# Routing steps at other tiles, the next run's first gathers ahead of the last scatters, and a third bank of line sums, in a fused two-layer mixer kernel

## The reference

```
x = x + _L0_conv_ref(_ln_c(x), ...)      # line convolutions, batch norm, one gate per image and channel
t = t + _L0_ffn_ref(_ln_t(t), ...)       # 8 experts, top 2 of the softmax, gelu (tanh)
x = x + _L1_conv_ref(_ln_c(x), ...)      # max pools of 7 sizes, two of them weighted per channel
t = t + _L1_ffn_ref(_ln_t(t), ...)       # 8 experts, top 2, gelu (erf)
```

## Time and profile before

| | us |
|---|---|
| three runs | 1142.77, 1144.22, 1144.31 |
| the profiled execution | 1153.62 |
| its span, first to last instruction | 1151.9 |
| PE busy | 821.9 (71%) |
| POOL busy | 625.4 (54%) |
| DVE busy | 566.6 (49%) |
| ACT busy | 527.0 (46%) |

### The profile page before, as it was taken

How to read it: one execution, slowest core, us unless ns; L and a number is a source line. 1 busy time by engine, 2 the same in 40 slices (tenths; PEclk the granted TensorE clock), 3 DMA queues, 4 the chain that set the end, 5 groups by cost and what they waited for, 6 DMA issues and landing times.

```text
span 1151.9 us, 14717 instructions
## 1 busy us (share of the span) xinstructions
PE 821.9 (71%) x4289; PEld 696.3 (60%) x4289; DVE 566.6 (49%) x1296; ACT 527.0 (46%) x1439; POOL 625.4 (54%) x598
## 2 busy tenths in 40 slices
PE   1754388887778776877688388776878877877670
PEld 0434267775677565765587277665768755666670
DVE  8877912270500291999557769997571003200004
ACT  1505054453445354544448166443575534444463
POOL 1000255666666674778733645787455666666551
PEclk9975599997988978998879689989887988889795
DMA  7001343442556752444234743444265646546356
GB/s 309 1 0 55 120 152 111 134 151 93 188 152 201 236 176 90 147 132 124 92 95 162 271 153 124 134 119 132 67 201 157 197 123 218 172 132 209 112 159 219
DMA packets 55391, 167.63 MB, mean 146 GB/s; under 512 B 13888, under 2 KB 13901, under 8 KB 55056
## 3 DMA queue, kind: packets, MB, share of 16 engines
q1 hardware_dynamic: 36880, 130.98, 34.0%
q0 software_dynamic: 18432, 35.70, 10.9%
HBM read 137.26 MB, written 31.46 MB: 146 GB/s over the span
## 4 chain that ended last, share of the span: by engine, by line
PE 49%; issue 14%; ACT 10%; another core or an unknown queue 8%; POOL 7%; DVE 6%; DMA 5%; SPq 0%; POOLq 0%; ACTq 0%; DVEq 0%
PE yT_ps L766 17%; PE h_ps L753 17%; PE turn_ps L688 4%; POOL xg L491 4%; DMA xg<-xn_rows,tile_rows 4%; POOL y_rows L500 3%; ACT hT L566 3%; PE acc_ps L705 3%; PE xT_ps L742 2%; ACT work L604 2%; PE yr_ps L776 2%; PE h_ps L851 1%; PE acc_ps L725 1%; ACT yT L577 1%
## 5 line engine op out<-in xcount | busy, mean ns | idle before, releaser
L500 POOL DMA_INDIRECT y_rows<-yr,tile_rows x288 | 313.1, 1087 | 280.3 <-ACT yr L586 201.1
L491 POOL DMA_INDIRECT xg<-xn_rows,tile_rows x288 | 308.1, 1070 | 221.9 <-DVEq L1168 130.1
L753 PE MATMUL h_ps<-xT,expert 128*128 128x256 f32 (+1 forms) x1408 | 321.0, 378 | 64.9 <-issue 47.3
L766 PE MATMUL yT_ps<-hT,expert 128*128 128x256 f32 (+1 forms) x1408 | 309.2, 372 | 40.6 <-ACT yT L577 28.4
L566 ACT ACTIVATE hT<-h_ps,expert 128x256 f32<-128x256 f32 (+1 forms) x704 | 254.8, 449 | 151.1 <-PE h_ps L753 72.8
L753 PEld LDWEIGHTS h_ps<-xT,expert 128*128 128x128 f32 x1408 | 249.0, 213 | 100.2 <-issue 66.8
L766 PEld LDWEIGHTS yT_ps<-hT,expert 128*128 128x128 f32 x1408 | 254.8, 212 | 77.5 <-ACT yT L577 33.4
L1202 DVE SCALAR_TENSOR_TENSOR tok<-work,share,tok 128x128 f32<-128x128 f32 x224 | 61.1, 346 | 328.5 <-DMA work<-y_rows 323.5
L577 ACT ACTIVATE yT<-yT_ps,expert 128x256 f32<-128x256 f32 (+1 forms) x176 | 73.9, 442 | 180.9 <-PE yT_ps L766 104.5
L742 PE MATMUL xT_ps<-ident,xg 128*128 128x128 f32 x288 | 62.7, 302 | 82.8 <-DMA xg<-xn_rows,tile_rows 72.2
L554 ACT ACTIVATE xT<-xT_ps 128x256 f32<-128x256 f32 x144 | 56.1, 390 | 139.7 <-PE xT_ps L742 94.1
(11 more groups left out here) (206 smaller groups left out, 642.7 us busy)
## 6 DMA issues: line engine op xcount, KB each, us to landing
expert<-in_experts SPq DMA_DIRECT2D x176, 514.5 KB
work<-y_rows SPq DMA_DIRECT2D x24, 512.0 KB, 9.5
xn_rows<-work SPq DMA_DIRECT2D x16, 512.0 KB, 2.7
xg<-xn_rows,tile_rows POOLq DMA_INDIRECT x288
y_rows<-yr,tile_rows POOLq DMA_INDIRECT x288
tok<-in_x_tokens SPq DMA_DIRECT2D x8, 512.0 KB, 7.1
state<-in_x SPq DMA_DIRECT2D x2, 2048.0 KB, 17.1
work<-y_rows SPq DMA_DIRECT2D x16, 256.0 KB, 6.0
```

The lines of the kernel that those rows point to most:

```text
L491: pool.indirect_dma_start(xg[:, s, h, :], None, xn_rows[unit], bass.IndirectOffsetOnAxis(ap=tile_rows[unit % 2][:, at, 0, h:h + 1], axis=0)) \
L500: pool.indirect_dma_start(y_rows[unit], bass.IndirectOffsetOnAxis(ap=tile_rows[unit % 2][:, at, 1, h:h + 1], axis=0), yr[:, s, h, :], None ...
L753: mm = pe.matmul(h_ps[c // 2][:, c % 2, cols], expert[:, t.load(h) % W_RING, c * P:(c + 1) * P], xT[:, t.slot(2), cols], start=True, stop= ...
L766: mm = pe.matmul(yT_ps[:, cols], expert[:, t.load(h, d) % W_RING, HIDDEN + c * P:HIDDEN + (c + 1) * P], hT[:, s, c, cols], start=(c == 0), ...
```

## The change

Four things are changed together.

1. **First pass.** ACT normalises groups 3 and 7 of image 0 and groups 1, 4 and 7 of image 1 (`BY_SCALAR`), all of an image ahead of its copies; DVE does the other 11. The product of image 0 with the line weights is no longer reduced by DVE but summed on PE in the bank `yT_ps`, as the column products are; its eight slabs are 8 neighbouring columns of each of the 64 lines. The product of image 1 is still reduced by DVE and now lies in the memory of `expert`.
2. **Drain of a run.** In step 35 PE and ACT take `turn_y` and `copy_rows` of tile 33 and of tile 34, in step 36 those of tile 35; step 37 holds no more work for them.
3. **POOL between the runs.** Tiles 0 and 1 of the next run are gathered in step 36 ahead of the scatters of tiles 34 and 35; tiles 2 and 3 follow after them. The waits for `s_rows` and `s_xn_st` move up with the first two.
4. **The table.** `mixing(0)`: route from 28.6 and 29.3 to 28 and 28.3, slots from 32 to 30.3, rows from 31..34 to 30..33, invert from 35.6..38 to 33..34.3. `mixing(1)`: read from 0 to 2, state and norm two tiles later, route, slots and rows 1.3 to 2.4 tiles later, invert 0.3 to 1.3 tiles later.

```diff
-    mixing(0, read=3, state=(6, 7, 7.6, 8), norm=11, route=(28.6, 29.3), slots=32, rows=(31, 32.6, 33, 34),
-           invert=(35.6, 36.6, 37, 38)),
-    mixing(1, read=0, state=(2, 2.6, 3, 4), norm=5, route=(23.6, 24.3), slots=26.6, rows=(26, 27, 27.6, 28),
-           invert=(29, 30, 30.6, 31)),
+    mixing(0, read=3, state=(6, 7, 7.6, 8), norm=11, route=(28, 28.3), slots=30.3, rows=(30, 31, 31.6, 33),
+           invert=(33, 33.3, 34, 34.3)),
+    mixing(1, read=2, state=(4, 5, 5.6, 6), norm=7, route=(25, 25.6), slots=28, rows=(27.3, 28.6, 29.3, 30),
+           invert=(30.3, 30.6, 31, 31.3)),
...
+    def drains(self):
+        return self.last <= self.s <= self.last + 1
...
+            def begin(u, ahead):
+                pool.wait_ge(s_rows, u + 1)
+                pool.wait_ge(s_xn_st[u], 16 * QUARTERS)
+                for d in ahead:
+                    gather(Tile(u, 0), d)
+
             for u in range(UNITS):
                 if begins_run(u):
-                    pool.wait_ge(s_rows, u + 1)
-                    pool.wait_ge(s_xn_st[u], 16 * QUARTERS)
-                    for d in range(G_AHEAD):
+                    if u == 0:
+                        begin(u, range(G_FIRST))
+                    for d in range(G_FIRST, G_AHEAD):
                         gather(Tile(u, 0), d)
...
+                    if t.s == t.last + 1 and u + 1 < UNITS:
+                        begin(u + 1, range(G_FIRST))
                     if t.has(-2):
                         scatter(t, -2)
...
-                    if t.has(-2):
+                    if t.has(-2) and t.s <= t.last:
                         turn_y(t, -2)
+                    if t.drains():
+                        turn_y(t, -1)
...
+            pe.wait_ge(s_mul, 1)
+            add_slabs(h_ps[0][:].rearrange("p a s -> p (a s)"), lambda g: tok_flat[0][:, g * chunk:(g + 1) * chunk])
+            pe.wait_ge(s_mul, 2)
+            add_slabs(yT_ps[:].rearrange("p (h w) -> p h w", h=SIDE),
+                      lambda g: by_row[0][:, :, g * SIDE // GROUPS:(g + 1) * SIDE // GROUPS])
+            pe.wait_ge(s_mul, 3)
+            add_slabs(h_ps[1][:].rearrange("p a s -> p (a s)"), lambda g: tok_flat[1][:, g * chunk:(g + 1) * chunk])
```

More of the change, by code:

```diff
@@ L59 @@
 G_AHEAD = 4
+G_FIRST = 2
 RUNS = [(0, 1), (2, 3)]
+BY_SCALAR = [(3, 7), (1, 4, 7)]
+BY_VECTOR = sum(GROUPS - len(groups) for groups in BY_SCALAR)
 AFTER_UP, AFTER_DOWN = 0.3, 0.6
@@ L293, in build @@
         yr = sb("yr", [P, RING, HALVES, P])
+        by_row = [m.rearrange("p (h w) -> p h w", h=SIDE)
+                  for m in (work[2][:], expert[:].rearrange("p w e -> p (w e)")[:, 0:TOKENS])]
         def one_hots(u, k):
@@ L647, in _ @@
             for b in range(IMAGES):
-                for g in range(GROUPS + 1):
-                    if g < GROUPS:
-                        if g % 2:
-                            for t in range(g * GROUP, (g + 1) * GROUP):
-                                i = b * BLOCKS + t
-                                ins = act.activation(tok[b][:, t, :], tok[b][:, t, :], ACT.Identity,
-                                                     bias=first_shift[:, i:i + 1], scale=first_rstd[:, i:i + 1])
-                            ins.then_inc(s_ln_odd, 1)
-                    if g:
-                        copy_group(work[b], g - 1)
+                for g in BY_SCALAR[b]:
+                    for t in range(g * GROUP, (g + 1) * GROUP):
+                        i = b * BLOCKS + t
+                        ins = act.activation(tok[b][:, t, :], tok[b][:, t, :], ACT.Identity,
+                                             bias=first_shift[:, i:i + 1], scale=first_rstd[:, i:i + 1])
+                    ins.then_inc(s_ln_act, 1)
+                for g in range(GROUPS):
+                    copy_group(work[b], g)
             turned.n += 2
@@ L832, in _ @@
             mm.then_inc(s_turned, 1)
+            by_scalar = [0]
             def turn_first(b):
                 for g in range(GROUPS):
-                    if g % 2:
-                        pe.wait_ge(s_ln_odd, (b * GROUPS + g + 1) // 2)
+                    if g in BY_SCALAR[b]:
+                        by_scalar[0] += 1
+                        pe.wait_ge(s_ln_act, by_scalar[0])
                     else:
@@ L981, in _ @@
             for b in range(IMAGES):
-                for g in range(0, GROUPS, 2):
+                for g in range(GROUPS):
+                    if g in BY_SCALAR[b]:
+                        continue
                     for t in range(g * GROUP, (g + 1) * GROUP):
@@ L992, in _ @@
                 banks_read(dve, turned.n)
[L993 removed]
+                img, by_h = (m.rearrange("p (h w) -> p h w", h=SIDE) for m in (work[b][:], tok_flat[b]))
                 dve.tensor_tensor(by_h, img, bc(conv_w[:, 0, :].unsqueeze(2), [P, SIDE, SIDE]), ALU.mult).then_inc(s_mul, 1)
[L995 to L1000 removed]
+                ins = dve.tensor_tensor(by_row[b], img, bc(conv_w[:, 1, :].unsqueeze(1), [P, SIDE, SIDE]), ALU.mult)
+                if b == 0:
+                    ins.then_inc(s_mul, 1)
+                else:
+                    op(ins)
+            op(dve.tensor_reduce(lines[:, 1, 1, :], by_row[1], AX.X, ALU.add))
+            summed = ((lines[:, 0, 0, :], h_ps[0][:].rearrange("p a (h w) -> p w (a h)", w=SIDE)),
+                      (lines[:, 1, 0, :], yT_ps[:].rearrange("p (h w) -> p h w", h=SIDE)),
+                      (lines[:, 0, 1, :], h_ps[1][:].rearrange("p a (h w) -> p w (a h)", w=SIDE)))
+            for n, (line, slab) in enumerate(summed):
+                dve.wait_ge(s_sum, n + 1)
+                op(dve.tensor_reduce(line, slab, AX.X, ALU.add))
             for k in range(2):
```

22 lines of the change are left out of this document (7 added, 15 removed).

## The result

| | before | after |
|---|---|---|
| runs, us | 1142.77, 1142.79, 1144.22, 1144.31 | 1125.38, 1126.26, 1127.53, 1127.80 |
| median | 1143.51 | 1126.89 |
| profiled execution, its span | 1153.62, 1151.9 | 1127.53, 1125.8 |

The ratio is 0.985, with a 95% interval of 0.9815 to 0.9884: 16.6 us faster, at 1126.9 where I had forecast 1125. The two traces are 26.1 us apart, since the profiled execution of before was 10 us over its own median and that of after is at its median. The ratios of the experiments leave out the few executions in a second, slower state, and one of `first_only` that took 4156 us.

What follows compares the result with a forecast made beforehand. POOL sets the pace inside a run wherever nothing stalls, with stalls on top, longest at routing steps and between runs. 3.4 - 17 - 5.5 = -19.1 us takes 1151.9 to 1132.8, execution 1134.5; scaled by 0.992, 1125 us, range 1113 to 1137.

Steps and rivals of the forecast that it cites:

- First pass: Image sums at the start: PE becomes the bound with three sums, the third ending at 68.9 against 65.51, +3.4 us.
- The strided sum: First pass, new sum on PE: plain column price taken; rival of 2.3 times the price, +10.1 us, 1135 us, 10 in 100.
- End of run 0: Routing of unit 2 leaves the path: `s_rows` at 614 to 620 instead of 640.1, scatter of tile 33 at 628.
- The rival without stalls: End of run 0: tile 33 scattered at 620, all 8 us earlier, 1117 us; 14 in 100.
- slots at 30.3 answer at once: End of run 0: DVE's slots find the top 2 ready, where it waited 10.03 us for them before.
- POOL and combine: Between the runs: 5.2 us of gathers come in between, combine starts at 647.6 instead of 645.85, costing DVE's chain 1.8 us.
- DVE's result: Unit 2: the result comes 40.6 us after the start of combine instead of 46.8, 6.2 us earlier.
- ACT stays late: Unit 2: the 10.21 us of idle and the stalls of the halves remain, -7.2 us, 1137 us; 12 in 100.
- The 12.4 us for two more tiles: Unit 2: two more tiles are through at DVE's result, 2 x 6.2 = 12.4 us gained.
- the 17: Unit 2 and its start: 12.4 + 6.2 - 1.8 = 17 us gained.
- Routing halves of unit 2: Halves at 25 and 25.6 stall POOL less than at 23.6 and 24.3: 5.5 us gained, bounds 0 and 11.
- End of the kernel and `s_rows` of unit 3: End of the kernel: 0, bounds +0.5 and -0.5; POOL's request for `s_rows` in step 32: 0, at most +2.

Runs made afterwards that it cites:

- before_again: The kernel before, unchanged, profiled a second time; ratio 1.0005 to the kernel before.
- first_only: The kernel before with the new first pass alone (table, drains and POOL of before); ratio 0.9982 to the kernel before.
- mixing0_old: The kernel after with the old table row of unit 1, all else new; ratio 0.9979 to the kernel before.
- no_pool: The kernel after without the early gathers ahead of the scatters of tiles 34 and 35; ratio 0.9837 to the kernel before.
- g_first_4: The kernel after with four tiles of unit 2 gathered ahead of the last scatters instead of two; ratio 0.9886 to the kernel before.

## Why the prediction was right, and where it was not

The sum was -19.1 us. In the table above the means of after's two traces and of those of before (with `first_only` from A on) differ by -1.1 us at the first gather, -6.6 in A, -8.9 in B, -1.9 in C and -1.2 in the last column; the other two are the same within 0.3. The two pairs of spans differ by 19.3 us on average, the timed runs by 16.6. The total is right and rests on errors that cancel: that it came so close is luck.

**First pass: wrong in sign**, +3.4 forecast (+1 at the least), -1.4 measured. The step that failed is "one takes 15.67/2 = 7.8 us". The row behind it mixes two paces. PE's groups in the trace of before, the first window (49.7 to 53.5 us) and the second (53.7 to 65):

```profile
L851 PE MATMUL h_ps<-tok,ident 128*128 128x512 f32 x5 | 4.1, 982 | 0.0
```

```profile
L851 PE MATMUL h_ps<-tok,ident 128*128 128x512 f32 x28 | 12.3, 595 | 0.0
```

The first four products start 0.85 us apart, those of the second window 0.43: the first run at TensorE's lower level. Before them PE had turned blocks with a pause of 1.37 us after every eight, 0.213 us from one to the next within the eight, the pace of the turns in after while the granted clock is 0.50 (0.109 at 1.00). In after it turns six groups almost without a pause, and the clock rises before the sums begin. These are windows of PE in after (length, busy, then the granted clock, 0.50 being 1.2 GHz and 1.00 being 2.4 GHz):

```profile
38.20:40.20 2.00, 1.93 (x9) 0.50 0.00 0
40.20:42.00 1.80, 1.80 (x9) 0.56 0.00 0
42.00:43.20 1.20, 1.05 (x9) 1.00 0.00 0
43.20:50.00 6.80, 6.80 (x18) 1.00 0.01 2
```

So each sum was 0.93 us shorter than I took, 2.8 us for three, and the last turn ended 2.1 us earlier, at 43.4. Together that is the 4.9 us between 68.9 and 64.0.

**The strided sum: right** to be taken at the plain price. It takes 7.03 us like the others, not 17.9. The rule of the Trainium skill (SBUF — State Buffer, Door 1: The DMA port swizzle), by which eight neighbouring fp32 numbers are read at full speed, agrees here. That rival is refuted, and the row behind it was misread. In the trace of before the passes of L725 start 0.13 us apart, and each has a weight load of its own:

```profile
L725 PEld LDWEIGHTS acc_ps<-hot_blocks,shared x128: 111/117/132, 120.7 to 858.4; 128*128 128x128 bf16 x128
```

The loads (111, 117 and 132 ns: lowest, median, highest) fill nearly all of that time, so the row gives the pace of loads and products together and no price for a stride.

**End of run 0: right in direction, too small.** Top 2 at 575.1 and 577.8 in the two traces (578 forecast), last table at 603.1 (602), `tile_rows` at 613.0 and 616.5 (614 to 620): the chain of the routing is as I worked it out. The step that failed is "the scatter of tile 33 is now at 630.36; I take 628". It came at 618.4 and 621.7. A is 86.3 us on average in before's two traces and `first_only`, 79.8 in after's two: 6.6 us, where I had 2.4. The rival without stalls put it at 620, and of this place it was the better account. The other traces bear it out. With the old row of unit 1 all four have A at 83.3 to 90.3 us and a long stand without a releaser at the second routing half: 6.35 us on PE in before, and 6.15, 9.15 and 6.44 us on ACT at one and the same instruction in `before_again`, `first_only` and `mixing0_old`. With the new row nine of ten have A at 78.6 to 81.1 and no such stand of PE or ACT over 3.3 us. The tenth, `no_pool`, with the same instructions in A, has 90.3 without such a stand. The granted clock in A does not tell them apart: 0.80 to 0.85 with the old row, 0.83 in `no_pool`, 0.83 to 0.92 in the nine. So the stand went with the row as a rule; what makes it, and what made `no_pool` long, stays open.

One reading was wrong though it did no harm: "slots at 30.3 answer at once". DVE still waits 5.66 us. PE's products were through by 576.0, and DVE reads at 581.25. The same part was there before: products until 596.9, read at 601.2, so 4.3 of the 10.03 us were never a wait for PE. In `g_first_4` the same pair of instructions took 0.48 us. What holds DVE there has no releaser in the trace and stays open.

**POOL and combine: right.** From scatter 33 to combine 19.7 us were forecast (15.5 + 5.2 - 1), 19.6 and 18.9 measured.

**DVE's result: wrong by 6.4 us.** The step "the result comes at 40.6" after combine; it came after 47.0 and 48.1, as before (46.8, 48.2). I had PE at step 7 some 32 us after combine and the copies right behind the turns. In ACT's timeline of after

```profile
672.11 0.39 ACT L571 ACTIVATE xT<-xT_ps 128x256 f32<-128x256 f32 x1 [1.54 <-remote]
675.03 0.84 ACT L583 ACTIVATE hT<-h_ps,expert 128x256 f32<-128x256 f32 x2 [2.54 <-remote]
676.42 0.84 ACT L583 ACTIVATE hT<-h_ps,expert 128x256 f32<-128x256 f32 x2 [0.55 <-remote]
...
677.77 0.62 ACT L561 ACTIVATE work<-turn_ps 128x512 f32<-128x512 f32 x1
...
684.24 0.59 ACT L561 ACTIVATE work<-turn_ps 128x512 f32<-128x512 f32 x1
```

ACT stands still for 4.1 us ahead of tile 6's activations, its waits having no releaser in the trace (before has such a pair in the same place, 2.29 and 2.52 us); PE turned the first groups from 672.7 on, ACT comes to them at 677.8, and eight copies with their sums take 7 us behind that. That was my rival "ACT stays late": the idle time stayed (8.57 us, not below 5), and so did the stalls of the halves, below. Its mechanism came true as a whole; its 1137 us did not, since the first pass and the end of run 0 gave more than its sum had. The 12.4 us for two more tiles came: at the result POOL has sent the scatters of five tiles instead of three. Measured for the two terms together: the result 7.6 us earlier and 12.4, or 20 us of lead in the first pair of traces; A and B as means, 15.5 against the 17 that I had. The 7.6 do not come from unit 2, though: they are the 12.0 us by which scatter 33 is earlier, less 4.1 by which combine follows it later and 0.3 of the chain behind that. The 17 were nearly met because A gave 6.6 where they held 2.4, while the 6.2 of an earlier result behind combine did not come.

**Routing halves of unit 2: -5.5 forecast, nothing shown.** The step that failed is to take one stall for something that the place of the step removes. POOL in C, before and after's second trace:

```profile
L500 POOL DMA_INDIRECT y_rows<-yr,tile_rows x40 | 43.7, 1092 | 42.9 <-ACT yr L586 32.1 <-issue 10.8
```

```profile
L509 POOL DMA_INDIRECT y_rows<-yr,tile_rows x40 | 45.5, 1137 | 41.0 <-ACT yr L603 29.5 <-issue 11.5
```

The wait for PE's and ACT's routing work is there at either place, 32 us and 30 us; only the first trace of after had 23.7.

**End of the kernel and `s_rows` of unit 3: 0 forecast,** and 210.3 and 210.5 us against 210.3 to 213.3 agree with that.

## What to carry to other kernels

Where one engine's chain sets a stretch, ask how many units of work the other engines have behind them at each of its points: early weights and two tiles more ahead of `norm` together took 12 us off B (103.7 to 92.0), while DVE's result stayed 47 us behind the start of combine. A move of a request ahead of other work pays only with its condition met early: with the late routing POOL stood 8.5 us at the moved wait, the scatters behind it. And never halve a grouped row to get a price: look at the first and the last of its instructions, since the pace can change inside it.
